# A four-layer graph network with two batches in flight: value products, turned rows and one output bank moved on TensorE

## The reference

```python
# layer 0
h = relu(layernorm(x))
agg = eps * h + adj @ h
x = x + silu(rmsnorm(agg @ W1 + b1) * w) @ W2 + b2          # hidden 1024
# layer 1
h = relu(layernorm(x)); g = h @ W.T + b
att = sigmoid(g @ a1 [:, None] + g @ a2 [None, :] + att_b) * adj * masks
x = x + (att / (sum(att, -1) + 1e-8)) @ g * mask
# layer 2, 8 heads of 32
h = relu(layernorm(x)); q, k, v = h @ Wq.T, h @ Wk.T, h @ Wv.T
s = q @ k.T / sqrt(32) + adj * We[head];  s = where(adj, s, -inf)
x = x + (softmax(s) @ v) @ Wo.T
# layer 3
h = relu(layernorm(x)); d = (sum(adj, -1) + 1e-5) ** -0.5
x = x + (d * adj * d) @ (h @ W3) + b3
```

## Time and profile before

| | us |
|---|---|
| median of 3 runs | 3715.15 |
| lowest and highest | 3715.06, 3717.53 |
| the profiled execution | 3719.9 |
| its span, first to last instruction | 3716.5 |
| mean granted clock of TensorE, as a share | 0.994 |
| TensorE busy | 3535.2 (95%) |
| VectorE busy | 2649.1 (71%) |
| ScalarE busy | 2291.3 (62%) |
| GpSimd busy | 775.1 (21%) |
| one step of the loop | 113.28 |

### The profile page before, as it was taken

One profiled execution on the slowest core, in us unless ns is written; L12 is line 12 of the kernel. 1 busy time (PEld: TensorE's weight loads), 2 busy tenths in 40 slices (PEclk: granted clock), 3 DMA queues, 4 the chain that ended last, 5 costly groups with the idle time before them and its releaser, 6 DMA issues.

```text
span 3716.5 us, 68617 instructions
## 1 busy us (share of the span) xinstructions
PE 3535.2 (95%) x20108; PEld 2488.2 (67%) x20108; DVE 2649.1 (71%) x6474; ACT 2291.3 (62%) x5062; POOL 775.1 (21%) x1611
## 2 busy tenths in 40 slices
PE   5999999999999999999999999999999999999997
PEld 4666667666667666667666666666776666766664
DVE  5777777777777777777777767777777777777764
ACT  3666566665666665666656666656666556666554
POOL 1122221222221222211222212222112222122210
PEclk8999999999999999999999999999999999999999
DMA  2233223232232332232322322322323222223212
GB/s 92 52 91 84 70 67 79 63 91 68 68 85 53 89 86 73 62 86 56 91 72 70 79 67 75 91 68 65 88 51 91 78 70 73 76 66 91 68 52 63
DMA packets 166941, 275.09 MB, mean 74 GB/s; under 512 B 23909, under 2 KB 59877, under 8 KB 166761
## 3 DMA queue, kind: packets, MB, share of 16 engines
q1 hardware_dynamic: 166760, 273.45, 27.7%
HBM read 122.37 MB, written 16.78 MB: 37 GB/s over the span
## 4 chain that ended last, share of the span: by engine, by line
PE 52%; DVE 15%; issue 14%; ACT 9%; POOL 6%; DMA 2%; SPq 1%; POOLq 0%; DVEq 0%; ACTq 0%
PE turn L1253 9%; PE value L1268 7%; PE front L1066 5%; PE score L1243 5%; PE score L1244 5%; PE front L1067 5%; PE front L1068 5%; PE front L1096 3%; ACT pT L615 3%; POOL small L398 3%; DVE pT L845 3%; PE front L1119 2%; DMA qk_stack<-qk 2%; POOL x_out L464 2%; ACT prob L606 2%
## 5 line engine op out<-in xcount | busy, mean ns | idle before, releaser
L606 ACT ACTIVATE prob<-prob,small 128x512 f32<-128x512 f32 x1024 | 736.5, 719 | 413.5 <-DVE small L921 411.8
L921 DVE CUSTOM_DVE_ANT_0 prob<-score,adj_sb,drv 128x512 f32<-128x512 f32 x1024 | 759.3, 746 | 169.6 <-PE score L1244 158.1
L1253 PE MATMUL turn<-ident,prob 128*128 128x128 f32 x4096 | 614.3, 275 | 14.9 <-ACT pT L615 8.2
L1253 PEld LDWEIGHTS turn<-ident,prob 128*128 128x128 f32 x4096 | 482.2, 141 | 110.3 <-issue 27.9
L1243 PE MATMUL score<-qk_stack 128*128 128x512 f32 x1024 | 488.7, 485 | 55.7 <-DMA qk_stack<-qk 36.3
L615 ACT ACTIVATE pT<-turn 128x512 f32<-128x512 f32 x768 | 447.3, 585 | 111.3 <-PE turn L1253 111.2
L1244 PE MATMUL score<-unlinked,neg_mask 128*128 128x512 bf16 x1024 | 399.6, 390 | 0.0
L1066 PE MATMUL front<-w_hi,s_hi 128*128 128x256 f32 x1024 | 355.8, 347 | 13.0 <-DVE drv L746 8.1
L705 DVE TENSOR_TENSOR s_lo<-front,s_hi 128x512 fp32r<-128x512 f32 x320 | 219.3, 685 | 128.1 <-ACT s_hi L510 128.0
L1067 PE MATMUL front<-w_lo,s_hi 128*128 128x256 f32 x1024 | 289.0, 282 | 0.0
L1068 PE MATMUL front<-w_hi,s_lo 128*128 128x256 f32 x1024 | 288.1, 281 | 0.0
(11 more groups left out here) (175 smaller groups left out, 7791.5 us busy)
## 6 DMA issues: line engine op xcount, KB each, us to landing
qk_stack<-qk SPq DMA_DIRECT2D x1024, 128.0 KB, 2.4
adjT_f<-in_adjT SPq DMA_DIRECT2D x32, 1024.0 KB, 5.3
adj_sb<-in_adj SPq DMA_DIRECT2D x32, 1024.0 KB, 7.3
prob<-in_adjT SPq DMA_DIRECT2D x32, 1024.0 KB, 5.3
x_new<-in_x SPq DMA_DIRECT2D x32, 512.0 KB, 4.1
out<-x_out SPq DMA_DIRECT2D x32, 512.0 KB, 3.0
pT<-in_W SPq DMA_DIRECT2D x2, 1024.0 KB, 11.0
rmsw_b<-in_rmsw SPq DMA_DIRECT2D x1, 512.0 KB
```

The lines of the kernel that those rows point to most:

```text
L606: act.activation(prob[:, i % 8, :], prob[:, i % 8, :], ACT.Exp, bias=nmax[:, h, n:n + 1], scale=-1.0, accum_out=prsum[:, h, n:n + 1]).then ...
L921: dve.tensor_tensor_reduce(out=prob[:, i % 8, :], in0=SB_[i % 2][:, :], in1=adj_sb[:, n, :], scale=neg_w[:, h:h + 1], scalar=3e38, op0=ALU ...
L1253: last = pe.transpose(TB[k % 2][:, tile(n)], prob[:, (4 * h + n) % 8, tile(j)], ident[:, :])
```

## The change

Three things on TensorE; no other engine's list is changed.

1. The second half of the values is computed in two pieces. `project_v` takes the pieces to make; piece 0 (six matmuls) now stands behind `hidden(tf, 0, 1)`, ahead of score product 0, with the wait for ScalarE's first copy. Piece 1 stays at g = -2.
2. In steps with both halves, `turn_hidden` of tile 0 stands behind `turn_probs` at g = 1 and g = 2.
3. `project3` writes tile 3 into FB[2]. In steps with a front its wait for VectorE's first addition becomes a wait for `msg_ready` of tile 1 of batch tf. The q projection of the next batch waits for the first addition of the batch before instead of all four, the k projection newly for the third, and the first `down` of a batch newly for all four of the batch before.

```diff
         def proj3_bank(n):
-            return (SB_[0], VB, SB_[1], SB_[0])[n][:, 0:D]
+            return (SB_[0], VB, SB_[1], FB[2])[n][:, 0:D]
...
             def down(tf, n, q):
                 pe.wait_ge(s_lo_ready, at(tf, 8, 2 * n + c + 1))
+                if q == 0 and n == 0 and (not isinstance(tf, int) or tf > 1):
+
+                    pe.wait_ge(out_ready, at(tf, 4, -4))
...
             def project_qk(t, g, i):
                     pe.wait_ge(bT_dve, at(t, 2, 2))
                     if later(t):
 
-                        pe.wait_ge(out_ready, at(t, 4, 0))
+                        pe.wait_ge(out_ready, at(t, 4, -3))
+                elif later(t):
+                    pe.wait_ge(out_ready, at(t, 4, -1))
...
-            def project_v(t, j):
-                if j:
+            def project_v(t, j, parts=(0, 1)):
+                if j and 0 in parts:
                     pe.wait_ge(v_ready, at(t, 2, 1))
-                elif later(t):
+                elif not j and later(t):
 
                     pe.wait_ge(o_ready, at(t, 2, 0))
-                for i in range(2):
+                for i in parts:
                     for k in range(DT):
...
-                last.then_inc(v_ps, 1)
+                if 1 in parts:
+                    last.then_inc(v_ps, 1)
...
-            def project3(t):
+            def project3(t, tf):
...
                 for n in range(2, NT):
-                    if n == 3:
-                        pe.wait_ge(out_ready, at(t, 4, 1))
+                    if n == 3 and tf is not None:
+                        pe.wait_ge(msg_ready, at(tf, 4, 2))
+                    elif n == 3:
+                        pe.wait_ge(out_ready, at(t, 4, 0))
...
             def phases(t, tf, nx, shared=None):
                 if f:
                     hidden(tf, 0, 1)
+                if b:
+                    project_v(t, 1, (0,))
...
-                            elif u in (5, 6):
+                            elif u in (5, 6) and not (b and n == 0):
                                 turn_hidden(tf, n, u - 5)
...
                     if b and g == -2:
-                        project_v(t, 1)
+                        project_v(t, 1, (1,))
...
                     if b and g >= 0:
                         turn_probs(t, g // 4, g % 4)
+                    if b and f and g in (1, 2):
+                        turn_hidden(tf, 0, g - 1)
...
                 if b:
-                    project3(t)
+                    project3(t, tf)
```

## The result

The changed kernel takes 3684.04 us as the median of 4 runs (3683.47 to 3685.76), beside 3716.34 us (3715.06 to 3718.31, 4 runs) for the kernel before: a ratio of 0.9912, 95% interval 0.99 to 0.9923. The gain of 32.3 us compares with a forecast of 38.4, and the time lies inside the range. The profiled execution took 3683.56 us, with a span of 3681.6, 34.9 less than before.

A forecast was written before the change was run, and what follows sets the result against it. The prediction took TensorE, busy 95% of the span, as the bound. 0.55 + 0.64 + 0 = 1.19 us a step gave 36.9 in 31 steps; with 1.5 for the last, 3715.15 - 38.4 = 3676.8 us, range 3662 to 3699.

The forecast's parts named there:

- The step: One loop step with both halves: 0.55 + 0.64 + 0 = 1.19 us less, from 113.28 to 112.1 us.
- the values: Six value products fill the hole ahead of score product 0; bias 2 comes 0.58 to 0.69 us sooner, taken as 0.64.
- the projection: Output projection's tile 3 in another bank: the stop for VectorE's first addition and its slow restart go, 0.55 us a step.
- the turns: Tile 0's hidden-row turns behind those of the probabilities: the stop moves ahead of the k projection; taken as 0, bounds -0.44 to 0.85.
- The chain: From the aggregation behind the output projection to score product 0, all links hang on TensorE and move forward whole by 0.55 us.
- the last rival: TensorE's gain is given back at a link such as SyncE's stacking issues: no change, 3710 to 3715 us; chance 0.07.
- The signs that I named: In TensorE's timeline: waits for `hid` shrink by some half or more; a new `qk` wait up to 0.4 us, 31 times.
- The waits that were added: Relaxed q projection wait, new ones at k projection and first `down`: taken at nothing, bound 0 to 0.1 us each.
- The dearer case: On TensorE, satisfied waits always stop early weight loads: three waits take back some 0.3 us a step, 9 us in all.
- The loop's turn (D): Rival: TensorE's loop turn becomes exposed like VectorE's, 1.46 to 1.99 us in each of 29 steps; slower, 3734.5 us; chance 0.05.
- The end and the start: Last step, without a front: half of the twelve value products hide in its 6.13 us stop; 1.5 us added to the gain.

The follow-up runs named there:

- e2: The kernel before with only the second half of the values cut in two pieces: 3702.43 us, ratio 0.9956.
- e1: The kernel before with only the output projection's bank and the waits that go with it changed: 3701.99 us, ratio 0.9955.
- e3: The kernel before with only tile 0's hidden-row turns put behind the turns of the probabilities: 3718.71 us, ratio 1.0.
- e4: The changed kernel with the hidden-row turns of tile 0 back in their old place: 3685.3 us, ratio 0.9907 to the kernel before.
- e7: The changed kernel with all twelve value products of the second half ahead of score product 0: 3688.93 us, ratio 0.9922 to the kernel before.
- e8: The changed kernel with the second k projection behind the turns at g = 3 and VectorE's low part of that k behind bias 9: 3666.05 us.
- e10: e8 with the hidden rows of tile 0 turned ahead of the probabilities, as in the kernel before: 3675.83 us, ratio 0.9889 to the kernel before.
- e11: The changed kernel with the next batch's q projection waiting for all four additions again: 3686.54 us, ratio 0.9919 to the kernel before.
- e9: The changed kernel with only VectorE's low part of the second k moved behind bias 9: 3679.88 us, ratio 0.9899 to the kernel before.
- e5: The changed kernel with the second k projection put behind the turn of the probabilities at g = 3: 3681.55 us, ratio 0.9903 to the kernel before.
- e12: e8 with ScalarE's second tanh of hidden tile 0 ahead of the copy of the first turned probabilities: 3664.81 us, ratio 0.986 to the kernel before.

## Why the prediction held, and where it didn't

**The step.** The forecast was 1.19 us less in each, and by the median it is 1.19. Its terms: the values brought 0.57 for 0.64 (e2), the projection 0.49 alone (e1) and at most 0.59 in the changed kernel, for 0.55, the turns nothing (e3, and S0 to T1 in e4). In the changed kernel one size came out smaller than forecast and the other larger. That the sum is exact is partly luck.

**The projection.** The mechanism was right, and its price depends on the kind of step. The prediction took 0.118 us for a distance of two products from the value products; the projection's own start 0.113 apart ahead of the stop in 20 of 28 steps of the kernel before. Seven of these are 0.79, so the stop cost 1.38 - 0.79 = 0.59 us in such a step, and T1 to P fell by 0.59 (77.96 to 77.37). In a step of the long kind it fell by 0.51 (77.98 to 77.47). With 23 short steps in 28 the median shows the first, in e1 with 13 a value near the second.

**The values.** The step that was mis-sized is the distance of bias 2 behind score product 2. I took it between 0.82, as behind a running TensorE, and 0.93, as behind a stop, and chose the middle. The score product comes 0.70 sooner behind score product 0, as worked out (2.44 to 1.74), at the very moment at which bias 0 is seen (1580.55 + 0.82 = 1581.37), and its own start is that of a stop: it is 0.49 long for 0.40 in the earlier trace rows, its bias follows in 0.93. So 0.70 - 0.11 = 0.59 less, 0.57 by the medians, the lower end. e7 shows that nothing more is to be had there.

**The chain.** That the 0.55 of the projection moves the whole chain to score product 0 forward was right: P to S0 is 12.07 before and 12.08 after, and score product 0 stands 1579.62 - 1566.99 = 12.63 behind the first product of tile 3, for 12.77. SyncE's side, where the last rival would have given the gain back, took none of it: the step's parts behind score product 0 are all as long as before or shorter.

**The turns.** The mechanism was right: an order in which the k projection waits for `qk_low` makes the new place worth nothing, and e8 with e10 gives its price when that is changed, 0.36 to 0.41. The signs that I named were off in size. I said that the waits for `hid` would shrink by half or more: they fell from 30.5 to 23.0, since only the stop ahead of the first turn was filled. The 0.39 a turn was too high as well: three waits in the first 75 us of the trace, 6.1, 2.0 and 2.0 us long, are part of the 30.5, and what is left is 0.33 for each of the 62, as in the earlier trace rows. Between the two turns lies the same work as before, so the second still comes too early; it starts 6.05 behind bias 2 in both kernels (1600.94 - 1594.89 and 1588.34 - 1582.29), when its `silu` is done. The new wait for `qk` is 0.22 a step and not 0.4, by the same cause. The stops of this stretch were 0.24 and 0.41 and are 0.42 and 0.22: 0.65 became 0.64.

**The waits that were added.** Taken at nothing, with 0.1 for each as the bound. e11 puts all four additions back into one of them and finds at most 0.07, and the product that follows the new wait on `msg_ready` starts 0.12 behind its forerunner. The new waits of the k projection and of the first `down` have no run of their own; the list of TensorE's waits in the changed kernel has none for `x_out`. By the rule of the Trainium skill that the prediction weighed (TensorE: Matmul & The Clock Gate, Step-by-step: what each phase is for), weight loads run ahead of the matmuls. The weight loads (PEld) show both cases, the changed kernel's behind `msg_ready` first, then that of the kernel before behind `x_out`:

```profile
1566.88 0.19 PEld L1066 LDWEIGHTS front<-w_hi,a_hi 128*128 128x128 f32 x1
```

```profile
1578.85 0.19 PEld L1066 LDWEIGHTS score<-w_hi,a_hi 128*128 128x128 f32 x1 [0.49 <-DVE x_out L969]
```

Where the wait is met already, the load starts 0.11 us ahead of its product (1566.99), under the product before, and agrees with the page; behind the real wait it starts 0.01 ahead (1578.86). The dearer case, in which every wait would stop the overlap, isn't seen.

**The loop's turn (D).** VectorE's turn costs the same as before, 1.96 us of standing idle for 1.99. TensorE's didn't come out from under its aggregation: the q projection follows 3.03 us behind its start (1567.67 to 1570.70), as before. The rival is out.

**The end and the start.** The last step gave 1.38 us, as taken (1.5), and the one before it 2.16, 1.0 more than its 1.19. The 29 steps at 1.14 lack 1.4 us. The stretch up to the first store holds one changed step too and should have come out 1.2 shorter; it came out 1.76 longer, 3.0 short, which the last section lays to the start. 38.4 - 1.4 + 1.0 - 0.1 - 3.0 = 34.9, the span's difference. The profiled times differ by 36.3, as less lies around the span of the second (2.0 for 3.4); and the profiled execution before stood 3.6 above the median of its runs, that after 0.5 below: 36.3 - 3.6 - 0.5 = 32.2, measured 32.3.

## What to carry to other kernels

A stop is worth filling only up to the point at which the next thing that the engine waits for is ready by another chain: look for the next wait behind it, and ask which engine sets it. The signature is one that any trace has: the distance between two events of the *other* engine doesn't change while your stops move. Where work and chain are about equally long, edits that give next to nothing one by one can give much together (by S0 to T1: the turns 0, e9 0.10, e5 0.12, all three 0.56), so try them crossed before you drop them. Measure a small edit in the stretch that it changes, since the rest of the step has a spread of its own (e9's 0.10 doesn't show in the step). And fill a stop of an engine with no more than fits in it: six products fit, twelve made score product 0 come 0.26 us later.

## What the hardware showed that was not expected

**The start differs from one execution to the next.** The first sixteen products of the aggregation are the same in both kernels and begin at the same moment. Timeline of TensorE, before and then after:

```profile
11.35 8.59 PE L1096 MATMUL front<-adjT_f,hid 128*128 128x512 f32 x16 [11.35 <-DVE adjT_f L782]
```

```profile
11.35 9.76 PE L1096 MATMUL front<-adjT_f,hid 128*128 128x512 f32 x16 [11.35 <-DVE adjT_f L782]
```

And the stages behind them (columns as in the earlier trace rows), before and then after:

```profile
21.00:60.00 39.00, 23.86 (x112) 19.82 (x112) 20.96 (x44) 13.25 (x24) 6.55 (x13) 0.82 0.14 47
60.00:120.00 60.00, 45.77 (x199) 31.44 (x199) 35.59 (x88) 24.53 (x45) 13.36 (x24) 0.89 0.10 29
```

```profile
21.00:60.00 39.00, 24.83 (x106) 20.42 (x106) 20.89 (x43) 13.85 (x25) 5.06 (x12) 0.74 0.14 48
60.00:120.00 60.00, 46.37 (x201) 32.49 (x200) 34.32 (x88) 23.26 (x43) 13.37 (x24) 0.86 0.07 21
```

Within the sixteen, the products start 0.85 us apart until 14.04 in the one and until 16.60 in the other, and 0.43 apart from 14.63 and from 17.09 on: half the pace first and then the full one, as at the two levels of the clock (1.2 and 2.4 GHz). The granted clock behind the first 21 us, a mean of stretches at these two levels, is lower in the second execution as well (0.74 for 0.82, 0.86 for 0.89). Over the fourteen kernels profiled the first store lies anywhere from 221.9 to 226.2 us, and goes along with this clock more than with any edit: 221.9, 222.3 and 222.4 in the kernel before, e9 and e2, all three with 0.82 and 0.89; 223.67 in the changed kernel; 226.2 in e7, with 0.74 and 0.80, the lowest. One execution of each kernel was profiled, so how far a single kernel's own start varies isn't shown. What sets the clock's course there isn't shown either. A time of the whole run so carries up to some 4 us that are the start's, as much as or more than e5, e9, e11 and e12 differ by from the kernels that they are changed from. The step's parts, taken from 28 steps of one trace, tell them apart where the whole time can't.

**Some steps are 0.3 us longer.** In the changed kernel three of 29 distances are 112.35 to 112.37, beside a median of 112.03; what is longer in them is P to S0, up to 12.4 for 12.08, at whose end score product 0 waits for its DMA. Before, four were 113.40 to 113.47 for 113.22. Why a landing is late now and then isn't shown.
